# Self attention with the products with values of two units at once, four exponentials buffers, and three small transfers issued by ScalarE

## The reference

```python
x = x + cross_attention(layernorm(x), ctx)     # 16 heads of 16, 120 keys, layer 0
x = x + moe_block(layernorm(x))                # self attention, 16 heads, 256 keys (layer 1),
                                               # then a choice of 1 of 8 experts for each token
x = x + cross_attention2(layernorm(x), ctx)    # layer 2
x = x + sets_block(layernorm(x))               # groups of 32 tokens sorted into 128 small networks
# every attention:
scores = einsum('bhqd,bhkd->bhqk', q, k) * tau + delta
out    = einsum('bhqk,bhkd->bhqd', softmax(scores / 4), v) @ Wo + bo
```

## Time and profile before

| | |
|---|---|
| median of 3 runs | 986.18 us |
| profiled execution | 987.44 us, span 985.6 us |
| layer 0 with its start, about | 0 to 218 us |
| self attention, items 8 to 15, about | 218 to 422 us |
| end of the block and routing | 422 to 480 us |
| experts | 480 to 694 us |
| layer 2 with its start | 694 to 854 us |
| sets | 854 to 985.6 us |
| mean granted TensorE clock | 0.877 of full speed |

### The profile page before, as it was taken

One profiled execution on the slowest core, in us unless ns is written; L12 is line 12 of the kernel. 1 busy time (PEld: TensorE's weight loads), 2 busy tenths in 40 slices (PEclk: granted clock), 3 DMA queues, 4 the chain that ended last, 5 costly groups with the idle time before them and its releaser, 6 DMA issues.

```text
span 985.6 us, 16486 instructions
## 1 busy us (share of the span) xinstructions
PE 804.3 (82%) x6167; PEld 611.9 (62%) x6167; DVE 502.9 (51%) x1231; ACT 349.6 (35%) x659; POOL 245.5 (25%) x258
## 2 busy tenths in 40 slices
PE   2567989989999999941599999955378898896998
PEld 2445766656666666531599999944266676675865
DVE  3355576776778676224122121225556876444743
ACT  1324553444454444510122222204044555533211
POOL 1513242232233232112211111024333542112000
PEclk9768998899999999965699999977577999857999
DMA  5768454855453565336545556333934460332001
GB/s 149 99 78 190 82 97 59 107 82 67 64 115 71 68 129 163 109 108 70 190 161 186 190 169 185 124 90 69 116 71 80 78 102 17 129 157 87 2 33 54
DMA packets 80376, 103.30 MB, mean 105 GB/s; under 512 B 35078, under 2 KB 70406, under 8 KB 75134
## 3 DMA queue, kind: packets, MB, share of 16 engines
q1 hardware_dynamic: 77882, 97.06, 44.3%
q0 software_dynamic: 2416, 5.19, 2.7%
HBM read 56.60 MB, written 7.28 MB: 65 GB/s over the span
## 4 chain that ended last, share of the span: by engine, by line
PE 64%; DVE 12%; DMA 8%; ACT 5%; issue 5%; POOL 4%; SPq 3%; DVEq 0%; POOLq 0%; ACTq 0%
PE PS L681 9%; PE U L692 8%; PE U L598 8%; PE MB L531 6%; PE MB L609 5%; PE MB L619 4%; PE PS L584 4%; PE MB L561 4%; PE MB L761 3%; PE MB L547 2%; PE MB L771 2%; DVE nma L1027 2%; DMA Oa<-Uba 2%; DMA y<-yb,pos 2%; PE PS L782 2%
## 5 line engine op out<-in xcount | busy, mean ns | idle before, releaser
L1027 DVE TENSOR_REDUCE nma<-MB 128x2 f32<-128x512 f32 (+1 forms) x192 | 124.2, 672 | 48.1 <-PE MB L561 47.4
L857 ACT ACTIVATE Pa<-PS 128x1024 f32<-128x1024 f32 (+1 forms) x96 | 97.4, 1023 | 69.2 <-PE PS L584 68.4
L1262 POOL TENSOR_TENSOR mv<-mv,vec 128x2 f32<-128x2 f32 x48 | 34.8, 725 | 248.6 <-DVE mv L982 248.4
L561 PE MATMUL MB<-QKa 99*128 99x120 bf16 (+1 forms) x512 | 74.4, 262 | 26.8 <-DVE nma L1027 11.5
L598 PE MATMUL U<-Pa,Vaa 128*32 128x256 f32 (+1 forms) x768 | 93.8, 410 | 0.9 <-ACT Pa L857 0.7
L681 PE MATMUL PS<-mzT,mw 128*128 128x128 f32 x736 | 88.3, 280 | 1.8 <-ACT mzT L878 1.8
L681 PEld LDWEIGHTS PS<-mzT,mw 128*128 128x128 f32 x736 | 86.3, 196 | 2.4 <-issue 2.3
L692 PE MATMUL U<-mw,mdT 128*128 x368 | 84.9, 384 | 2.3 <-DVE mdT L1166 2.3
L561 PEld LDWEIGHTS MB<-QKa 99*128 99x128 bf16 x512 | 40.6, 105 | 61.2 <-issue 21.1
L692 PEld LDWEIGHTS U<-mw,mdT 128*128 128x128 f32 x368 | 69.2, 193 | 11.5 <-issue 2.7
L1174 DVE TENSOR_TENSOR yt<-U,mb 128x256 f32<-128x256 f32 x23 | 9.8, 424 | 124.4 <-PE U L692 124.4
(11 more groups left out here) (194 smaller groups left out, 1456.1 us busy)
## 6 DMA issues: line engine op xcount, KB each, us to landing
mw<-in_mw SPq DMA_DIRECT2D x31, 1024.0 KB, 5.7
QKa<-spa SPq DMA_DIRECT2D x144, 128.0 KB, 5.1
QKb<-spb SPq DMA_DIRECT2D x48, 128.0 KB, 4.8
Oa<-Uba SPq DMA_DIRECT2D x16, 256.0 KB
v<-in_v SPq DMA_DIRECT2D x1, 4096.0 KB, 13.4
v<-in_v SPq DMA_DIRECT2D x4, 1024.0 KB, 11.7
W<-in_W SPq DMA_DIRECT2D x3, 1280.0 KB, 7.3
yb<-yt SPq DMA_DIRECT2D x23, 128.0 KB, 1.7
```

What stands on the lines that cost most here:

```text
L561: i = e.matmul(b[:, keys * j:keys * j + keys], Q[0:99, h0 + j, 128 * qt:128 * qt + 128], K[0:99, h0 + j, 0:keys], start=True, stop=True)
L857: e.activation(p[0:keys, :], ps[0:keys, :], ACT.Exp, scale=0.25).then_inc(sems["exp"], 1)
L1027: e.tensor_reduce(A.nm[qt][:, h0:h0 + heads], b[:, 0:heads * keys].rearrange("p (h s) -> p h s", h=heads), AX.X, ALU.max, negate=True).the ...
L1262: e.tensor_tensor(rs[r][:, 0:2], ve[r][:, 0:2], mhalf[:, 0:2], ALU.pow).then_inc(sems["rs"], 1)
```

## The change

The products with values of self attention are done for two units at once. In `pipeline()` a self item's `pv` stands only after each second unit; `values` issues the first key tile of the four heads in the four column groups, then the second key tile of all four. `PVS` and `PV_OF` count these steps for those who wait for them. Cross attention keeps its order and its products.

Self attention gets a fourth P buffer, in the last 8 KB of the region, where layer 0 keeps its context; the first exponential that uses it waits for the last reads of that context. The exponential of a unit waits for the pair that holds the unit four before.

The transfer of the maxima (L1430 before) and of the sums and rows (L1439, L1440) move from SP's list to ScalarE's, right behind the copies that they read, with all the waits they had on SP. Sums and rows get a semaphore each (`d_l`, `d_o`) in place of a shared one. VectorE's inverse waits for the sums alone.

```diff
         for h in range(2 * U):
             if h % 2 == 0:
                 out.append(("sc", n, h // 2))
-            elif h > 1:
+            elif h > 1 and (cross(n) or h % 4 == 1):
                 out.append(("pv", n, h // 2 - 1))
...
+PVS = [s[1:] for s in STEPS if s[0] == "pv"]
+PV_OF = [next(k + 1 for k, (n, u) in enumerate(PVS) if UNIT[n, u] >= unit) for unit in range(len(UNIT))]
+P_OF = [(unit - UNIT[8, 0]) % 4 if layer(n) == 1 else unit % 3 for (n, u), unit in UNIT.items()]
...
+            heads = [(exps(n, u), m, head) for m, head in enumerate(place(n, u))]
+            if tiles == 2:
+                heads = [(exps(n, u - 1), m, head) for m, head in enumerate(place(n, u - 1))] + heads
+            for kt in range(tiles):
+                for p, m, (half, gg, j) in heads:
                     c = 256 * (tiles * m + kt)
...
             e.activation(att(n).mT[n % 2][:, :], bank("mt", n)[0:32, 0:256], ACT.Identity).then_inc(sems["max_turned"], 1)
+            if n >= 4:
+                g.wait_ge(*ended(n - 4))
+            g.wait_ge("max_turned", n + 1)
+            e.dma_start(att(n).Qs[n % 4][99:101, :, :], att(n).mT[n % 2][:, :]).then_inc(sems[f"d_m{n % 4}"], 16)
...
             g.wait_ge("sc", unit + 1)
-            g.wait_ge("pv", unit - 2)
+            if (n, u) == (8, 3):
+                g.wait_ge("proj", SPLIT["kp", 7] + 1)
+                g.wait_ge("v_t", count("vp", 7))
+            if P_BEFORE[unit] is not None:
+                g.wait_ge("pv", PV_OF[P_BEFORE[unit]])
...
+                if half == 1:
+                    g.wait_ge("p2", n - 1)
+                    g.wait_ge("u_copied", 2 * (n + 1))
+                    e.dma_start(A.Lr[n % 2][:, :], ub[1:128:32, :, :, :].rearrange("p g h q -> p (g h q)")
+                                ).then_inc(sems[f"d_l{n % 2}"], 16)
+                    e.dma_start(A.O[n % 2][:, :, :], ub[0:128:2, :, :, :].rearrange("p g h q -> p g (h q)")
+                                ).then_inc(sems[f"d_o{n % 2}"], 16)
...
-        def max_rows(n):
...
-        def values(n, u):
```

More of the change, by code:

```diff
@@ L266 @@
 SPLITS = list(SPLIT)
+PVS = [s[1:] for s in STEPS if s[0] == "pv"]
+PV_OF = [next(k + 1 for k, (n, u) in enumerate(PVS) if UNIT[n, u] >= unit) for unit in range(len(UNIT))]
+P_OF = [(unit - UNIT[8, 0]) % 4 if layer(n) == 1 else unit % 3 for (n, u), unit in UNIT.items()]
+P_BEFORE = [max((k for k in range(unit) if P_OF[k] == P_OF[unit]), default=None) for unit in range(len(UNIT))]
 LOW = {(s[0][0] + "p", s[1]): k for k, s in enumerate(s for s in STEPS if s[0] in ("qs", "ks"))}
@@ L368, in __init__ @@
             self.P = m.ring(f"P{tag}_", 3, [128, 1024])
+            if ksw != CK:
+                self.P.append(Area(r_end - 8192, r_end).new(f"P{tag}_3", [128, 1024]))
             assert m.p <= r_end - (8192 if ksw != CK else 131072 - 98304)
@@ L443, in build @@
     names += [f"d_w1{i}" for i in range(3)]
-    names += ["d_o0", "d_o1"] + [f"d_{w}_{t}" for w in ("delta", "ctx", "ones", "dsx", "sel") for t in "ab"]
+    names += [f"d_{w}{i}" for w in "lo" for i in range(2)]
+    names += [f"d_{w}_{t}" for w in ("delta", "ctx", "ones", "dsx", "sel") for t in "ab"]
     sems = {name: stack.enter_context(nc.semaphore(f"s_{name}")) for name in names}
@@ L476, in ended @@
     def ended(n):
-        return "pv", UNIT[n, units(n) - 1] + 1
+        return "pv", PV_OF[UNIT[n, units(n) - 1]]
     def split_landed(k):
@@ L589, in values @@
             A, unit = att(n), UNIT[n, u]
-            V, p = A.Va[n % 4], A.P[unit % 3]
+            V = A.Va[n % 4]
             keys, tiles = (CK, 1) if cross(n) else (128, 2)
@@ L594, in values @@
             g.wait_ge("u_copied", 2 * n + place(n, u)[0][0])
-            for m, (half, gg, j) in enumerate(place(n, u)):
-                for kt in range(tiles):
+            heads = [(exps(n, u), m, head) for m, head in enumerate(place(n, u))]
[3 more added lines that the diff above has]
+                for p, m, (half, gg, j) in heads:
                     c = 256 * (tiles * m + kt)
@@ L861, in values @@
             if (gg, j) == (1, 3):
-                g.wait_ge("pv", UNIT[n, u] + 1)
+                g.wait_ge("pv", PV_OF[UNIT[n, u]])
+                A, ub = att(n), att(n).Ub[n % 2]
                 if half == 0 and n >= 2:
-                    g.wait_ge(f"d_o{n % 2}", 32 * (n // 2))
-                e.activation(att(n).Ub[n % 2][:, :, half, :], U[:, :].rearrange("p (g q) -> p g q", g=2),
-                             ACT.Identity).then_inc(sems["u_copied"], 1)
+                    g.wait_ge(f"d_l{n % 2}", 16 * (n // 2))
+                    g.wait_ge(f"d_o{n % 2}", 16 * (n // 2))
+                e.activation(ub[:, :, half, :], U[:, :].rearrange("p (g q) -> p g q", g=2), ACT.Identity
+                             ).then_inc(sems["u_copied"], 1)
+                if half == 1:
[5 more added lines that the diff above has]
+                                ).then_inc(sems[f"d_o{n % 2}"], 16)
         def gate_turn(n):
```

27 lines of the change are left out of this document (9 added, 18 removed).

## The result

The changed kernel takes 997.64 us (median of 4 executions, 994.53 to 1002.67), the kernel before beside it 985.3 us. The ratio is 1.0163, 95% interval 1.0119 to 1.0207: 1.6% slower, where 965 us were forecast. The profiled execution has a span of 994.0 us against 985.6, and a mean granted clock of 0.866 against 0.877.

The account below looks back on a forecast made before the run. PE was taken to bound self attention (busy 176.5 of 182 us). Terms -15 - 3 - 6 - 6 + 6.5 + 2 = -21.5 took 987.4 to 965.9, so 965 us for the median; 8 in 10 range 948 to 980.

Parts of the forecast that it names:

- A: Self attention, items 8 to 15: pairs of units save 32 us of PE work, of which 15 us arrive.
- B: Item 15's sums and rows, issued by ScalarE, no longer stand behind SP's transfers: -3 us, between -7 and 0.
- C: Item 0's rows, issued by ScalarE, come sooner and PE's wait of 4.49 us goes: -6 us, between -8 and 0.
- D: First maxima of layers 0 and 2, issued by ScalarE, land 3 to 4 us after issue: -6 us together.
- E: ScalarE is held by issuing the transfers, mainly in layers 0 and 2: +6.5 us, between 0 and +15.
- F: At item 23, v1's 4 MB load now goes before the copy and delays the rows: +2 us, between 0 and +10.
- rivals on VectorE: Self attention: VectorE takes PE's place, pinned stretches double, the pairs gain 6 us; 974 to 975 us, chance 0.13.
- the clock: Rival: self attention's granted clock falls to 0.90 and 9 us are lost; 974 us, chance 0.13.
- the 0.92: Sign of being wrong: a clock under 0.92 in the self attention stage.
- Issuing engines are not separate DMA queues: Skill section; read strictly, it gives the rival that the moved transfers gain nothing: 980 us, chance 0.10.
- The packet by packet rotation: Rule behind the transfer forecasts: DMA engines alternate between ScalarE's and SyncE's rings, so a small transfer waits a packet or so.
- The rival "slower": ScalarE's issues are on the path in all 16 cross items: 6 us slower, 992 us, chance 0.06.

Follow-up runs that it names:

- rows first: pairs only, with the last two expert-weight loads moved behind item 15's sums and rows in SP's list; 968.2 us, 0.9841 of the kernel before.
- pairs only: The changed kernel with the transfers of maxima, sums and rows back in SP's list, two semaphores kept; 972.7 us, 0.9908 of the kernel before.
- after: The changed kernel, with the whole change, against the kernel before; 997.64 us, ratio 1.0163.
- transfers only: The changed kernel with products and three buffers as before, the transfers still on ScalarE; 1000.7 us, 1.0182 of the kernel before.
- maxima on SP, loads held: The changed kernel with maxima back on SP, and SP's loads of expert weights and v1 waiting for their item's rows; 969.7 us, 0.9835 of the kernel before.

## Why the prediction was wrong, step by step

The forecast missed by 33 us. Part A missed by 4 to 8; the rest lies in the transfers. Their parts B to F were to gain 6.5 us together, and the transfers alone lost 18.4 by the spans (1004.0 against 985.6). By the table, of this gap of 25 us the issues on ScalarE (E; layer 0, items 8 to 15 and layer 2 lost 18.6 for the 6.5 forecast) make 12, the gains of B, C and D that did not come (7.2 for 15, over the start and the stretch behind item 15) 8, and the last stretch (F; 7.0 for 2) 5. These are differences of single traces.

**A, pairs: right in kind, over by 4 to 8 us.** A pair takes 1.0 us from its start to the next instruction, as taken from the earlier trace rows, and 29 of the 32 us of PE work went. Alone the pairs brought 11.4 us from item 7 to 15, 7.4 in rows first; I had -15. The waits for exponentials at the ends of items came as forecast (9 waits, 1.1 us at most); those for VectorE came to some 15 us, where before had 5, and so was the half clock (0.95 in pairs only and 0.93 in rows first, from 7 to 15, against 0.97). The rivals on VectorE and the clock, which I held apart, each came in part. In after the clock between 240 and 422 us was 0.91, under the 0.92 that the prediction had named as a sign of being wrong.

**B, item 15's rows: the size near, by another cause.** The reciprocal came 9.8 us after the copy instead of 12.2, 2.4 for the 3 forecast. But in pairs only, with the transfers on SP behind the same two loads, it came 8.45 us after the copy. And the rows themselves landed later from ScalarE; this is their time from issue to landing in after and in pairs only, where before had 10.70:

```profile
Oa<-Uba ACTq DMA_DIRECT2D x1, 256.0 KB, 13.9
```

```profile
Oa<-Uba SPq DMA_DIRECT2D x1, 256.0 KB, 11.0
```

So the output projection of item 15 began 16.3 us after the copy in after, 17.3 in before, 13.6 in pairs only, and 7.7 in rows first. After and pairs only share everything but the issuing engine there, so the move cost 2.7 us instead of bringing 3. What helps in the others is the semaphore of the sums (G), and in rows first the place of two loads in SP's list.

**C, item 0's rows: half came, and nothing shows that the move brought it.** The reciprocal comes 9.8 us after the copy where it was 12.3, and the stretch from copy 0 to copy 1 takes 17.9 us instead of 21.6, against 6 forecast. But the kernels with the rows on SP and the two semaphores have 9.0 to 10.9 us and 15.5 to 20.2 us there.

**D, first maxima: failed, nothing came.** The step said that they "should land 3 to 4 us after" on ScalarE. The chain of after at the start of layer 2:

```profile
703.33 6.70 DMA QKb<-mTb
```

It was 6.76, and PE waits 4.39 us for it, 4.45 before; in layer 0 it is 2.81 against 2.80. In the list of queues of after there is a new one with 7.08 MB, which is what ScalarE's 72 transfers move. Of its packets between 703.4 and 708 us there are none, while the old queue moves 672; between 708 and 711 us:

```profile
q1 hardware_dynamic: 99, 0.05, 10.0%
q10 hardware_dynamic: 34, 0.02, 2.8%
```

So the transfer has a queue of its own, and here it still went only when what was issued before it on the other was nearly through. It is not so everywhere. Between 863 and 867 us, with v1 under way, packets of both queues ran side by side, 56 of the old with 1.58 MB and 59 of ScalarE's with 0.08 MB, and the sums of item 23, at 870.88 at the latest, were there before the two loads of 1 MB that had been issued ahead of them (17.1 us after their issue, so about 873). One for one in packets is 1 to 20 in bytes there, and between 857.9 and 863 us ScalarE's queue had moved only 4 packets, the old one 65.

Of the two sections of the Trainium skill, DMA: Bandwidth & Descriptors, that I had set against each other, Issuing engines are not separate DMA queues (only issue time is saved) fits all four places: no run shows that the move brought any of their transfers sooner. The packet by packet rotation of its section on queues, rings and completion order fits the packets of 863 to 867 us, but not those of 703.4 to 708; and where it fits, it did not bring the small transfer in early, which is what B, C and D took from it. Why the packets wait in the one place and not in the other stays open.

**E, ScalarE held: the step that failed by most (+6.5 forecast, 18.6 in transfers only).** It said "In self attention ScalarE has slack (86.9 of 182), but for item 15". The slack is an average. At the start of an item ScalarE has a copy and an exponential to make, and PE comes for that exponential just as it is ready. With 1.2 us of issues in between and before's products, PE waited 9.6 us in 8 places, and the stage was 10 us longer, half of it at item 15 (where the overtaking loads have a share). With the pairs the loss is seen at item 15 above all, and in maxima on SP, loads held the whole stage takes 197.2 us, for 192.6 to 196.6 in the kernels with everything on SP. For layer 2 it said that an output projection hides the rows and that the maxima cost about 2 with item 16; the maxima cost 5 to 6 us there, through waits of 0.7 us and half clock behind them. The prices of an issue themselves were right as a rule (medians of 0.57 to 0.69 us on ScalarE, the longest 1.27), and so was that of layer 0, or somewhat low: from copy 1 to 7 it cost 3.9 us for the 4.4 of items 1 to 7, but before's 116.8 is at the top of the nine kernels with the rows elsewhere (112.7 to 116.8), and L543 waits for zTa in item 2 a little longer than the 1.3 to 1.6 us that were named:

```profile
115.58 1.99 PE L543 MATMUL MB<-zTa,W 128*128 128x256 f32 x8 [1.69 <-ACT zTa L816]
```

**F, loads that go first: the mechanism right, the count wrong.** For v1 I took +2; the last stretch took 4.7 us more, and 3.7 of it went when v1 was held. The prediction said of item 15 that the loads "leave ahead of the copy even now", and did not ask the same of items 13 and 14, where they had stood behind the rows. There, with item 15, holding the loads is worth 4.7 us to item 14, 1.6 to item 15 and 11 us to the stretch behind it. The last stretch varies by 3 us without any such load ahead (132.6 to 135.4 in the kernels with pairs and the rows on SP), so the 3.7 is little above that.

**G, a semaphore each for sums and rows: a part of the change for which the prediction has no term.** Before, the reciprocal of item 15 waited for the rows too; in pairs only it waits for the sums alone:

```profile
434.18 0.55 DVE L1043 RECIPROCAL La<-La 64x64 f32<-64x64 f32 x1 [9.50 <-DMA Oa<-Uba]
```

```profile
415.81 0.54 DVE L1066 RECIPROCAL La<-La 64x64 f32<-64x64 f32 x1 [5.91 <-DMA La<-Uba]
```

That is 3.8 us from the copy to the reciprocal, and as much to the projection. No kernel has this alone, so its share of the whole, and of the 0.9908 of pairs only, is open.

The rival "slower" had 992 us by ScalarE's issues in all 16 cross items. It came to 998, in part by that (items 2 to 4 of layer 0, items 19 to 21 of layer 2) and in part by what it did not name, the loads that overtook.

## What to carry to other kernels

To move the issue of a transfer to another engine takes away a place in a list, not the transfers ahead of it; look at what was kept behind it by the old list, since that now leaves first. Before an issue of 0.6 us goes to a computing engine, look at the instruction right behind it and who waits for that, not at the engine's share of busy time: at a later place, behind two exponentials, the same issues cost items 1 to 7 nothing. A semaphore that two transfers share makes the first one's reader wait for both. What TensorE saves where another engine stands close behind it comes back as waits, and the clock can fall behind a wait; here 7 to 11 of 29 us arrived.

## What the runs showed of the hardware

A short wait may be followed by far more than itself at the lower clock: one of 1.38 us by 10 us, one of 0.71 by some 6; and not every wait is. That the wait is the cause is argued, not shown. Pairs only and rows first have the same instructions in layer 2. In rows first, PE at item 22:

```profile
799.89 0.28 PE L583 MATMUL MB<-idb,Mhb 128*32 128x128 bf16 x2 [1.62 <-DVE Mhb L1061]
...
801.69 2.00 PE L625 MATMUL MB<-Lb,selb 64*128 64x64 f32 x16
```

and in pairs only:

```profile
808.64 0.28 PE L583 MATMUL MB<-idb,Mhb 128*32 128x128 bf16 x2 [1.59 <-DVE Mhb L1061]
...
811.73 3.67 PE L625 MATMUL MB<-Lb,selb 64*128 64x64 f32 x16
```

The same wait of 1.6 us, full clock behind the one and half behind the other, and item 22 is 4.7 us longer. The two differ before that wait already: from 796 to 804 us the granted clock of pairs only was 0.84 and 0.74, while rows first had 1.00 throughout. But in the 18 us up to there PE ran the same rows in both, with the same waits to 0.03 us, so the first fall of the clock has no cause in these rows. The stretch from 21 to 23 took 29.7, 31.5, 34.5 or 36.1 to 36.6 us in the kernels' traces, whatever the edit. One profiled execution is therefore not enough for a difference under some 7 us in this kernel.

Sums of 16 KB with 2 MB ahead of them on the other queue were ready 7 to 9 us after their issue, with 4 MB and twice 1 MB ahead 13 us; with 2 MB ahead on their own queue (item 15 of pairs only) 7.6 us. The price went by the bytes ahead, and nothing came sooner for standing on the other queue; the rows behind these sums even landed 13.9 us after their issue from ScalarE and 11.0 from SP.
